# Block-scaled FP4 feed-forward stages: who makes the scale that leads back, and where the block maximum is kept

## The reference, cut to what matters

```
def fp4_quant_dequant(x):                      # blocks of 16 along the last dim
    xb = x.reshape(shape[:-1] + (shape[-1] // 16, 16))
    scale = max(max(|xb|) / 6.0, 1e-12)
    xn = xb / scale
    q = nearest value of {0, .5, 1, 1.5, 2, 3, 4, 6} to |xn|, with its sign
    return q * scale
gate = fp4(x) @ fp4(w_gate).T                  # 128 -> 352
y    = fp4(x) @ fp4(w_up).T                    # 128 -> 352
h    = silu(gate) * y
out  = fp4(h) @ fp4(w_down).T                  # 352 -> 128
x    = x + 0.5 * out
```

## Time and profile before

| | |
|---|---|
| median of 3 runs | 1919.78 us (1916.09 to 1920.82) |
| the profiled execution: its own time | 1921.65 us |
| its span, first to last instruction | 1919.2 us |
| busy in the span | PE 88%, DVE 78%, PE weight loads 68%, ACT 52%, POOL 43% |
| TensorE granted clock, mean | 0.968 of full speed |

### The profile page before, as it was taken

How to read it: one execution, slowest core, us unless ns; L and a number is a source line. 1 busy time by engine, 2 the same in 40 slices (tenths; PEclk the granted TensorE clock), 3 DMA queues, 4 the chain that set the end, 5 groups by cost and what they waited for, 6 DMA issues and landing times.

```text
span 1919.2 us, 73934 instructions
## 1 busy us (share of the span) xinstructions
PE 1683.3 (88%) x31945; PEld 1306.7 (68%) x31945; DVE 1506.5 (78%) x3788; ACT 994.4 (52%) x2784; POOL 824.8 (43%) x875
## 2 busy tenths in 40 slices
PE   5999899997999678876999999999999999857897
PEld 4888677775888556665667777767666767635666
DVE  5786577765566699985888888888888888859997
ACT  2444333432344466644666566665566666536664
POOL 2000444442000177753454544454444545427876
PEclk9999899998999899997999999999999999969999
DMA  4000000000000000000000000000000000000001
GB/s 126 1 1 1 2 4 4 4 4 3 1 1 1 1 1 1 1 1 2 4 4 4 3 4 4 4 4 3 4 4 3 4 3 4 3 1 1 23 23 44
DMA packets 14625, 14.92 MB, mean 8 GB/s; under 512 B 1440, under 2 KB 12128, under 8 KB 14304
## 3 DMA queue, kind: packets, MB, share of 16 engines
q1 hardware_dynamic: 11104, 8.83, 1.6%
q10 hardware_dynamic: 3200, 1.37, 0.3%
HBM read 6.01 MB, written 4.19 MB: 5 GB/s over the span
## 4 chain that ended last, share of the span: by engine, by line
PE 59%; DVE 24%; issue 8%; POOL 4%; ACT 4%; DMA 1%; DVEq 0%; POOLq 0%; SPq 0%
PE acc L519 7%; PE acc L496 6%; PE acc L1889 4%; PE acc L1905 3%; DVE arena L1353 3%; PE acc L883 3%; DVE acc L1004 3%; DVE arena L1017 3%; DVE arena L1345 2%; DVE arena L994 2%; PE acc L510 2%; PE acc L1937 2%; PE acc L858 2%; PE acc L1921 2%; PE acc L1839 2%
## 5 line engine op out<-in xcount | busy, mean ns | idle before, releaser
L1041 POOL TENSOR_TENSOR arena<-arena 128x960 f32<-128x960 f32 (+2 forms) x74 | 177.5, 2398 | 312.0 <-DVE arena L1010 216.7
L1686 POOL TENSOR_TENSOR arena<-arena 128x288 f32<-128x288 f32 x192 | 143.6, 748 | 297.8 <-DVE arena L1345 239.9
L1692 POOL TENSOR_TENSOR arena<-arena 128x256 f32<-128x256 f32 x192 | 139.6, 727 | 107.0 <-ACT arena L1572 103.7
L469 ACT ACTIVATE arena<-acc,wib 128x256 f32<-128x256 f32 x256 | 100.5, 475 | 152.9 <-PE acc L510 152.9
L1572 ACT ACTIVATE arena<-acc 128x288 f32<-128x288 f32 x192 | 79.0, 412 | 178.9 <-PE acc L1911 176.6
L1905 PEld LDWEIGHTS acc<-arena 64*64 64x64 f32 x3072 | 110.7, 134 | 68.0 <-DVE arena L1366 65.3
L1905 PE MATMUL acc<-arena 64*64 64x72 f32 (+1 forms) x3072 | 136.7, 225 | 21.8 <-DVE arena L1366 20.0
L1127 PE MATMUL acc<-wguT,arena 128*128 128x352 f32 x256 | 105.2, 494 | 48.1 <-DVE arena L994 47.1
L1889 PE MATMUL acc<-arena 64*64 64x72 f32 x2560 | 116.9, 229 | 32.3 <-POOL arena L1692 32.2
L1889 PEld LDWEIGHTS acc<-arena 64*64 64x64 f32 x2560 | 95.5, 134 | 68.2 <-DVE arena L1359 50.1
L1911 PE MATMUL acc<-arena 64*64 64x72 f32 x3072 | 139.2, 230 | 0.0
(11 more groups left out here) (261 smaller groups left out, 4814.3 us busy)
## 6 DMA issues: line engine op xcount, KB each, us to landing
out_dram<-X SPq DMA_DIRECT2D x3, 1024.0 KB, 5.3
out_dram<-X SPq DMA_DIRECT2D x1, 512.0 KB, 3.2
wi<-in_wiT_dram ACTq DMA_DIRECT2D x1, 256.0 KB, 6.2
wout<-in_woT_dram ACTq DMA_DIRECT2D x1, 256.0 KB, 9.6
out_dram<-X SPq DMA_DIRECT2D x1, 256.0 KB, 2.3
out_dram<-X SPq DMA_DIRECT2D x2, 128.0 KB, 2.6
wqkv<-in_w_qkv_dram ACTq DMA_DIRECT2D x1, 192.0 KB, 6.8
arena<-in_w_down_dram SPq DMA_DIRECT2D x1, 176.0 KB, 4.9
```

What stands on the lines that cost most here:

```text
L1041: pool.tensor_tensor(b3(y[k][:, part(u)]), b3(z[k][:, part(u)]), each(small[u % kept][:, 1, blocks(u)]), ALU.mult).then_inc(y_ready, 1)
L1686: pool.tensor_tensor(tm[s][:, :, cols], sq[s][:, group[0], cols], rm[s][:, :, cols], ALU.subtract)\
L1692: pool.tensor_tensor(high[s], sq[s][:, group[1], 0:LM], unit[:, it, :].unsqueeze(1).broadcast_to([P, PG, LM]), ALU.add).then_inc(high_read ...
```

## The change

The block maximum gets a buffer of its own in the arena, `amaxs`, one of 60 values for each of the four units that are kept. DVE's reduction writes it there and raises a new semaphore, `max_ready`, in place of the step of the chain. DVE makes `top` from it as before, in the accumulator bank, and the reciprocal from `top`. The scale `scl` is no longer made by DVE: POOL makes it from `amaxs` with the same arithmetic, at the head of `scaled`, behind the wait for `half_ready` that stands ahead of `scaled` and in front of L1041. DVE waits, before it writes a maximum, until POOL has used the one four units earlier.

```diff
+            amaxs = [cut(NZ) for _ in range(kept)]
...
-            peak = psum[:, 7, 0:2 * kept * NZ].rearrange("p (u c b) -> p u c b", u=kept, c=2)
+            peak = psum[:, 7, 0:kept * NZ].rearrange("p (u b) -> p u b", u=kept)
...
                     if u < NB:
                         dve.wait_ge(xn_ready, u + 1)
-                    amax, top = (peak[:, u % kept, c, blocks(u)] for c in range(2))
-                    scl, inv = (small[u % kept][:, c, blocks(u)] for c in range(2))
-                    c = chain.did(dve.tensor_reduce(amax, b3(z[u % DEEP][:, part(u)]), AX, ALU.max,
-                                                    apply_absolute_value=True))
-                    chain.settle(c)
+                    if u >= kept:
+                        dve.wait_ge(scl_ready, u - kept + 1)
+                    amax, top, inv = amaxs[u % kept][:, blocks(u)], peak[:, u % kept, blocks(u)], small[u % kept][:, 1, blocks(u)]
+                    dve.tensor_reduce(amax, b3(z[u % DEEP][:, part(u)]), AX, ALU.max,
+                                      apply_absolute_value=True).then_inc(max_ready, 1)
+                    dve.wait_ge(max_ready, u + 1)
                     c = chain.did(dve.tensor_scalar(top, amax, (1.0 + 2.0 ** -22) / 6.0, 1e-12, ALU.mult, ALU.max))
-                    dve.tensor_scalar(scl, amax, 1.0 / 6.0, 1e-12, ALU.mult, ALU.max).then_inc(scl_ready, 1)
                     chain.settle(c)
                     dve.reciprocal(inv, top).then_inc(inv_ready, 1)
...
                 def scaled(u):
                     k = u % DEEP
+                    pool.wait_ge(max_ready, u + 1)
+                    pool.tensor_scalar(small[u % kept][:, 0, blocks(u)], amaxs[u % kept][:, blocks(u)], 1.0 / 6.0, 1e-12,
+                                       ALU.mult, ALU.max).then_inc(scl_ready, 1)
                     pool.wait_ge(inv_ready, u + 1)
                     pool.tensor_tensor(b3(y[k][:, part(u)]), b3(z[k][:, part(u)]), each(small[u % kept][:, 1, blocks(u)]),
                                        ALU.mult).then_inc(y_ready, 1)
```

More of the change, by code:

```diff
@@ L956, in fp4_ffn @@
             hq = [zq[s][:, HX:HZ].rearrange("p (j f) -> p j f", f=FH) for s in U]
-            xn_ready, inv_ready, scl_ready, y_ready, big_ready, half_ready, rnd_ready, zq_ready, xT_done, xqT_ready, gate_done, \
+            xn_ready, max_ready, inv_ready, scl_ready, y_ready, big_ready, half_ready, rnd_ready, zq_ready, xT_done, xqT_ready, gate_done, \
                 up_done, sig_ready, hid_ready, hT_done, hqT_ready, y_done, added = (
                     sem(f"{ph}_{n}") for n in (
-                        "xn_ready", "inv_ready", "scl_ready", "y_ready", "big_ready", "half_ready", "rnd_ready", "zq_ready", "xT_done",
+                        "xn_ready", "max_ready", "inv_ready", "scl_ready", "y_ready", "big_ready", "half_ready", "rnd_ready", "zq_ready", "xT_done",
                         "xqT_ready", "gate_done", "up_done", "sig_ready", "hid_ready", "hT_done",
```

## The result

The changed kernel takes 1940.85 us, median of 4 runs (1933.33 to 1945.22), against 1917.99 us for the kernel before, also over 4 runs by now. The ratio is 1.0114, with a 95% interval from 1.0078 to 1.0149. The profiled execution took 1945.22 us with a span of 1943.4 us, 24.2 us over the span of before.

The account below looks back on a forecast made before the run. It took a loop of L1017, L1020, L1041 and L1053 sharing one port as the bound; 5.5 us in the first FP4 stage, 7.3 in the last and 1.2, 0.4, 1.0 at the ends gave 15.4, hence 1935.2 us, range 1926 to 1945.

Parts of the forecast that it names:

- What bounds the stages: First FP4 and last stage: L1017, L1020, L1041 and L1053 take turns on one port, 5.67 us a round.
- L1008 worth 0.01 us: DVE's order: L1008 lies in a gap that stays, so removing it gains 0.01 us a unit; bound 0.13 or 0.21.
- the maximum's new memory: DVE's L1004 and L1007: writing and reading the maximum in the arena saves 0.01 us each, bounds 0 and 0.02.
- the place of the maximum and the new semaphores: DVE: the maximum in the arena, `max_ready` and the wait for `scl_ready` add no time.
- POOL's new instruction: POOL, ahead of L1041: delays L1041 and all behind it by 0.33 us a unit, bounds 0.19 and 0.60.
- the upper bound: POOL's new instruction: 0.60 us a unit, from 0.45 for two arithmetic steps plus a doubling of 152 ns for the values.
- the ends of the stages: Rounds outside the 22 steady ones, start-up and drain of both stages: 1.2, 0.4 and 1.0 us more.
- The other loop, through ACT: Last stage, through ACT's L1071 and L1004: 5.52 us after L1053's end against the lock's 5.67, so it stays below.
- the lock doesn't hold for the small instruction: POOL's new instruction runs while L1020 streams, under cover, leaving 1919 us; chance 0.12.
- DVE is the bound and L1008 counts in full: DVE bounds, the loop through POOL has slack: 8 us less, 1912 us; chance 0.04.
- the instruction is dear: POOL's new instruction costs 0.60 us a unit, rounds 6.27, 1948 us; from 0.45 on, 1941; chance 0.15.
- DVE's `top` would queue for the port: DVE's L1007, reading the arena, waits for L1053's end: about 0.7 us more a round, 1966 us; chance 0.04.

Follow-up runs that it names:

- e1_one_scale: Kernel before without L1008 and nothing put on POOL, one DVE instruction making one scale for both uses: 1914.41 us, ratio 0.9978.
- e8_act: Changed kernel with ACT instead of POOL making the scale, at the head of ACT's round, without the lower bound of 1e-12: 1913.87 us, ratio 0.9990 to before.
- e4_ahead: Changed kernel with POOL's new tensor_scalar moved ahead of its wait for `half_ready`: 1913.32 us, ratio 0.9983 to the kernel before.
- e2_ts_alone: Kernel before plus the new POOL tensor_scalar into an unused buffer, DVE's instructions unchanged but for one added wait: 1938.92 us, ratio 1.0107.
- e5_between: Changed kernel with POOL's new tensor_scalar between its two large instructions, `scaled` and `restore`: 1946.23 us, ratio 1.0169 to the kernel before.
- e7_dve_arena: Changed kernel with the scale back on DVE, read from and written to on-chip memory: 1932.26 us, ratio 1.0094 to the kernel before.
- e3_memset: Kernel before plus a POOL memset of 512 values a partition, which reads nothing, in the new instruction's place: 1916.56 us, ratio 0.9984.
- e9_ahead_twice: Changed kernel with POOL's tensor_scalar done twice ahead of the wait for `half_ready`, the second into an unused buffer: 1934.46 us, ratio 1.0096 to before.
- e10_ahead_wide: Kernel before plus a POOL tensor_scalar of 512 values a partition ahead of the wait for `half_ready`: 1969.22 us from two runs, ratio 1.0278.

## Why the prediction was right, and where it was off

**What bounds the stages** was right. The four instructions that take turns, L1017, L1020, L1041 and L1053, set the round of the last stage before, and of both stages after. A memset that does not read is free, a tensor_scalar that reads costs 0.49, two cost 0.98, and with one or two of them the rounds of both stages become equal: DVE's own order with its statistics, which needs 5.74 or 5.75, then lies under the loop.

**L1008 worth 0.01 us** was right: 0.01 to 0.02 in the changed kernel, e1_one_scale and e8_act. The further 0.02 that it gave DVE for the maximum's new memory don't show: with it e4_ahead and e8_act have first-stage rounds of 5.74, as e1_one_scale has without it, and not 5.72. That the place of the maximum and the new semaphores cost nothing was right too (e2_ts_alone gives the whole loss without them).

**The mis-sized term is POOL's new instruction:** 0.33 us a unit in the prediction, 0.49 measured. Two things make up the 0.16. The line through the earlier trace rows gave 0.36 for a duration that is 0.41 (e5_between): the instruction has two arithmetic steps where L1709 has one, which I named as an uncertainty and put in the upper bound alone (no run separates the second step from the rest). And I let the next instruction start 0.03 before the end, as L1053 does behind L1041, where it starts 0.08 behind it: 0.11 more. The 0.08 stood in the earlier trace rows, between two tensor_scalar instructions; I used it for the bound and not for the value. With 0.49 the sum is 22 * 0.41 + 22 * 0.49 = 19.8, and with the 2.6 that I had for the ends of the stages 22.4; the medians differ by 22.9.

That 1940.85 lies inside the range of 1926 to 1945 is in part luck. The rise was 22.9 us where I had 15.4, half as much again. The 1927 to 1941 of the forecast itself covers prices up to 0.45; the price was 0.49, the rival's region, and it was the base that came out 1.8 us lower beside the changed kernel (1917.99 against 1919.78) that kept the median just under 1941.

**The ends of the stages** were sized at 2.6 us. In the profiled executions they come to 5.6 between first and last `scaled` (11.5 - 9.0 and 13.9 - 10.8) and -1.2 outside (-1.3 + 2.0 - 1.9). A part of that is chance: in the drain DVE's L1021 and POOL's L1057 can collide or not. Before, a `restore` over 704 values took 2.03 instead of 1.39 in the last stage's drain; after, it is in the first stage's drain. Such a collision stands at another place from run to run, and no run says why. These differences were not followed up. Nor was the spread of the changed kernel's own runs, 0.6%.

**The other loop, through ACT,** stayed below, as said: in the last stage L1018 still starts ahead of L1057's end and stands until it. L1006 waits 0.18 us there, where L1004 waited 0.19 for ACT; the profile after doesn't name what ended the wait.

**The rivals.** That the lock doesn't hold for the small instruction is refuted, in the place of the change, by its 1.38 us. That DVE is the bound and L1008 counts in full is refuted by e1_one_scale. That the instruction is dear came closest; the measured price lies a little above the 0.45 where I drew the line between it and the forecast. That DVE's `top` would queue for the port is refuted (0.22 us after, 0.23 in the earlier trace rows), but e7_dve_arena shows the mechanism for the scale with both sides in on-chip memory: 0.64 and 1.15 us.

**What the prediction did not see:** it took the whole loop for occupied, "its place in the queue makes its price", and looked only at the place that the change gives it. Placed ahead of the wait for `half_ready`, the same instruction costs nothing (e4_ahead), because there it ends while POOL would have stood still behind L1020 anyway, and it holds DVE up by less than the rounds can show.

No version came out more than 0.22% below the kernel before, and e3_memset, whose rounds did not change, came out 0.16% below. The best that the experiments point to, e4_ahead and e8_act, are its equals: they save DVE 0.01 us a round, and 5.67 us stay with the four large instructions.

## What to carry to other kernels

When two engines share a port, look for instructions of the same kind and shape with two different durations, and add up what takes turns before counting busy time; that sum, not the busier engine, may be the round. The price of a small instruction moved onto the other engine is mostly fixed (here 0.30 of 0.49 us), and where it stands in that engine's queue decides whether it is paid at all: one wait further ahead it was free. Where an instruction's two sides lie can matter more than how much it moves: beside the same POOL instruction, 60 values took DVE 0.22 us from on-chip memory to the accumulator memory, 0.21 the other way, and up to 1.15 from on-chip memory to on-chip memory (e7_dve_arena; the 0.21 from the earlier trace rows).

## What was unexpected of the hardware

A POOL instruction over 60 values that already stood in wait for the port when DVE's first streaming instruction ended finished 0.26 us later, inside DVE's second, which kept its 1.16 us (e4_ahead; 0.07 us less than a lock over whole instructions would give). The same instruction begun 0.32 us into DVE's second was held until that one's end (e9_ahead_twice). Over 512 values in the first place it held DVE up by 0.29 us only and ran almost at its own pace (e10_ahead_wide). The Trainium skill (SBUF — State Buffer, SBUF: two separate sides) has the loser blocked until the other's whole instruction is over; the second of these three agrees with it, the third does not by 1.3 us, and the first does not by the 0.07 us alone. A small POOL tensor_scalar starts 0.08 us behind the end of the instruction before it and holds the next off by 0.08 us, while tensor_tensor instructions and the memset overlap their neighbours by 0.03 to 0.05 us.
